# Key chain ahead of h, h in the buffer of its own transposes, and one output tile in front of attention, in a two-layer linear-attention kernel

## The reference

```python
xn = _ln(x, ln_w, ln_b)
q = xn @ Wq + bq
k = xn @ Wk + bk + (1.0 - src_mask) * -1000000.0
q = softmax(q per head, over the head's features)
k = softmax(k per head, over the tokens)
v = (xn @ Wv + bv) * src_mask
att = jnp.einsum('bnhd,bnhl->bhdl', k, v)
y = jnp.einsum('bnhd,bhdl->bnhl', q, att)
scale, shift = jnp.split(jax.nn.silu(emb) @ W_emb + b_emb, 2)
hh = _ln(y, ln2_w, ln2_b) * (1.0 + scale) + shift
out = x + jax.nn.silu(hh) @ W_out + b_out
```

## Time and profile before

| what | value |
|---|---|
| median of three runs | 903.98 us |
| profiled execution, its own time | 908.92 us |
| span of the program in it | 907.1 us |
| PE busy | 822.0 us, 91% |
| DVE, ACT, POOL busy | 703.4, 514.4, 428.5 us |
| mean granted clock of PE | 0.96 |

### The profile page before, as it was taken

One profiled execution on the slowest core, in us unless ns is written; L12 is line 12 of the kernel. 1 busy time (PEld: TensorE's weight loads), 2 busy tenths in 40 slices (PEclk: granted clock), 3 DMA queues, 4 the chain that ended last, 5 costly groups with the idle time before them and its releaser, 6 DMA issues.

```text
span 907.1 us, 13792 instructions
## 1 busy us (share of the span) xinstructions
PE 822.0 (91%) x4871; PEld 424.2 (47%) x4871; DVE 703.4 (78%) x1410; ACT 514.4 (57%) x997; POOL 428.5 (47%) x418
## 2 busy tenths in 40 slices
PE   4995998899897998999999898989989898989987
PEld 2434444354453544545454544545454454536443
DVE  5987678568696786989886887868687886868976
ACT  4663774664456665777675665555564545551431
POOL 2251684525536555657473654344254444443240
PEclk9998899999899999999999998999999999999998
DMA  9588386745565656867495838567474847557451
GB/s 319 217 161 262 73 161 181 138 94 161 110 174 115 94 158 133 207 136 184 86 179 113 155 109 152 159 121 170 94 169 111 141 138 140 128 100 157 70 116 70
DMA packets 291093, 130.53 MB, mean 144 GB/s; under 512 B 261296, under 2 KB 261680, under 8 KB 291024
## 3 DMA queue, kind: packets, MB, share of 16 engines
q1 hardware_dynamic: 288000, 124.87, 60.5%
q10 hardware_dynamic: 3024, 4.78, 1.5%
HBM read 47.74 MB, written 16.88 MB: 71 GB/s over the span
## 4 chain that ended last, share of the span: by engine, by line
PE 64%; DVE 16%; issue 10%; ACT 6%; DMA 2%; SPq 1%; POOL 0%; DVEq 0%; ACTq 0%
PE ring L493 56%; PE att_ps L493 6%; DVE sb_kt_or_y L1024 2%; ACT sb_k_or_qt L1306 2%; DVE sb_row_peak L782 1%; DVE sb_kt_or_y L1018 1%; DMA sb_w_stage<-in_L_cond_Wk 1%; DVE sb_k_or_qt L930 1%; DVE sb_kt_or_y L1029 1%; ACT sb_kq_hi L1314 1%; DVE sb_w_lo L849 1%; DVE sb_y_stats L1006 1%; DVE sb_q_sum L983 1%; DVE ring L1002 1%; ACT sb_htok L1340 1%
## 5 line engine op out<-in xcount | busy, mean ns | idle before, releaser
L493 PE MATMUL ring<-sb_w_hi,sb_xt_parts 128*128 128x512 f16 x1024 | 316.4, 386 | 0.2 <-ACT sb_v_or_q L1363 0.2
L493 PE MATMUL ring<-sb_w_lo,sb_xt_parts 128*128 128x512 f16 x512 | 197.8, 386 | 0.0
L493 PEld LDWEIGHTS ring<-sb_w_hi,sb_xt_parts 128*128 128x128 f16 x1024 | 102.4, 100 | 131.4 <-issue 15.5
L493 PE MATMUL ring<-sb_w_hi,sb_ht_parts 128*128 128x512 f16 x512 | 158.0, 383 | 1.9 <-DVE sb_v_parts L940 1.9
L493 PE MATMUL ring<-sb_xt_parts,sb_w_hi 128*128 128x512 f16 x512 | 154.9, 385 | 0.0
L1533 POOL TENSOR_TENSOR sb_htok<-sb_kt_or_y,sb_htok 128x512 f16<-128x512 f32 x60 | 75.6, 1260 | 94.4 <-ACT sb_htok L1340 93.4
L1524 POOL TENSOR_TENSOR sb_x<-sb_x,sb_bias_o 128x512 f32<-128x512 f32 x64 | 79.1, 1270 | 81.9 <-DVE sb_k_or_qt L930 76.9
L1363 ACT ACTIVATE sb_v_or_q<-ring,sb_ln_one 128x512 f32<-128x512 f32 x64 | 43.9, 686 | 107.5 <-DVE ring L965 107.5
L1549 POOL TENSOR_TENSOR sb_tanh<-sb_v_or_q,sb_kq_hi 128x512 f16<-128x512 f32 x64 | 73.7, 1161 | 55.5 <-ACT sb_kq_hi L1368 54.5
L493 PE MATMUL ring<-sb_xt_parts,sb_w_lo 128*128 128x512 f16 x256 | 98.0, 383 | 0.0
L493 PE MATMUL ring<-sb_w_lo,sb_ht_parts 128*128 128x512 f16 x256 | 97.9, 383 | 0.0
(11 more groups left out here) (214 smaller groups left out, 1513.3 us busy)
## 6 DMA issues: line engine op xcount, KB each, us to landing
out<-sb_x SPq DMA_DIRECT2D x14, 1024.0 KB, 4.5
sb_rows_now<-film_rows SPq DMA_DIRECT2D x16, 512.0 KB, 4.7
sb_x<-out SPq DMA_DIRECT2D x8, 1024.0 KB, 5.4
sb_x<-in_x SPq DMA_DIRECT2D x7, 1024.0 KB, 5.4
sb_mask_add<-mask_terms SPq DMA_DIRECT2D x15, 256.0 KB, 5.7
sb_w_stage<-in_L_cond_Wk SPq DMA_DIRECT2D x2, 1024.0 KB, 9.3
sb_w_hi<-in_L_cond_W_emb SPq DMA_DIRECT2D x1, 1536.0 KB, 12.7
sb_w_lo<-in_L_cond_W_emb SPq DMA_DIRECT2D x1, 1536.0 KB, 13.5
```

Of the source, the lines that this page charges most:

```text
L493: last = nc.tensor.matmul(out, lhs, rhs, start=(n == 0), stop=(n == len(pairs) - 1))
```

## The change

- In `keys_beside_h` and `h_beside_keys` the chain of the keys (mask, maximum, exponent, sum, high and low half) goes first, and the gates and halves of h of the unit before come between and behind; values come after both.
- SP turns the keys first and h after them, and h's turning waits for all of h (`h_lo_ready`). The keys' turning waits for h no more, because Y, z and h of every unit but the last stand in `ht_parts`, the space into which h is turned (`y_of`).
- Tile 0 of the output of u-1 stands in front of attention on PE; tiles 1 to 3 stay behind it.
- Film products (unit 2) and shift products (units 3 to 5) move from behind value tiles to behind query tiles; `turn_film` moves behind O 0, `turn_table(1)` behind K 0 of unit 3.
- On POOL `add_bias` moves behind `low_queries` and `low_attention`.
- In unit 0: the first two key tiles begin with their hi·hi products, before the low halves are there; the query weights of layer 1 are split by ACT and POOL; `attention` is split by tiles of v and `mask_attention` by column block; peak, scale and split of W_out of layer 1 are in unit 0; half of the loads of layer 2's film weights moves to unit 1.

```diff
+        def y_of(u):
+            return kt_or_y if u == LAST else ht_f32
...
             def turn_h(u):
...
+                sp.wait_ge(h_lo_ready, 4 * u)
                 turn(ht_hi.rearrange("p t c m -> p (t c) m"), flat_h[0], h_hi_ready, 4 * u, ht_hi_ready)
...
             def turn_k(u):
                 if u == 0:
-                    sp.wait_ge(w_ready[0], 8)
-                    sp.wait_ge(shift_part, 2)
-                else:
-                    sp.wait_ge(h_lo_ready, 4 * u)
+                    sp.wait_ge(q0_ready, 1)
...
+                turn_k(u)
                 turn_h(u)
-                turn_k(u)
...
             def with_k(i):
-                    if u == 1 and i == 0:
-                        pe.wait_ge(table_copied, 2)
-                        sum_w(0, O_)
+                    if u == 3 and i == 0:
+                        turn_table(1)
...
+                pe.wait_ge(ht_hi_ready, 16 * u)
+                pe.wait_ge(ht_lo_ready, 16 * u)
+                output(u - 1, (0,), with_o)
                 if shifted is not None:
                     pe.wait_ge(shift_folded, folded(1, shifted))
                 pe.wait_ge(h_ready, 4 * u)
                 attention(u)
...
-                pe.wait_ge(ht_hi_ready, 16 * u)
-                pe.wait_ge(ht_lo_ready, 16 * u)
-                output(u - 1, between=with_o)
+                output(u - 1, (1, 2, 3), with_o)
                 attend(u)
...
             def keys_beside_h(u):
                 masked_keys(u, 0)
+                masked_keys(u, 1)
                 affine(u - 1, 0)
+                masked_keys(u, 2)
+                masked_keys(u, 3)
+                key_shift(u)
                 affine(u - 1, 1)
                 gate(u - 1, 0)
                 affine(u - 1, 2)
+                affine(u - 1, 3)
+                key_sums(u)
                 gate(u - 1, 1)
+                for i in range(C):
+                    low_keys(u, i)
                 gate(u - 1, 2)
                 gate(u - 1, 3)
...
                 attended_all(u)
+                if u == 2:
+                    film_scales(1)
```

More of the change, by code:

```diff
@@ L488, in take_bank, with product @@
                 return bank(name, i, unit)
-            def product(out, pairs, ahead=lambda n: None):
+            def product(out, pairs):
                 for n, (lhs, rhs) in enumerate(pairs):
-                    ahead(n)
                     last = nc.tensor.matmul(out, lhs, rhs, start=(n == 0), stop=(n == len(pairs) - 1))
@@ L600, in attention, with first_attention @@
                 last.then_inc(att_summed, 1)
+            def first_attention():
+                pe.wait_ge(kt_hi_ready, 16)
+                pe.wait_ge(kt_lo_ready, 16)
+                for tiles in (range(T - 1), (T - 1,)):
+                    pe.wait_ge(v_lo_ready, tiles[-1] + 1)
+                    for c in range(C):
+                        f = slice(c * P, c * P + P)
+                        for t in tiles:
+                            pairs = ((tile(kt_hi, c, t), v_hi[:, t, f]), (tile(kt_hi, c, t), v_lo[:, t, f]), (tile(kt_lo, c, t), v_hi[:, t, f]))
+                            for n, (lhs, rhs) in enumerate(pairs):
+                                last = nc.tensor.matmul(att_ps[:, c, :], lhs, rhs, start=(c == t == n == 0), stop=(c == C - 1 and t == T - 1 and n == 2))
+                last.then_inc(att_summed, 1)
             def attend(u, between=lambda t: None):
@@ L970, in mask_attention @@
                 dve.wait_ge(att_summed, u + 1)
+                if u == 0:
+                    for c in range(C):
+                        nc.vector.tensor_tensor(att[:, c, :], att_ps[:, c, :], blocks[:, 0, :], ALU.mult).then_inc(att_ready, 1)
+                    return
                 if layer:
@@ L1368, in high_queries @@
                 nc.scalar.copy(kq_hi[:, t * D:t * D + D], q[:, t, :]).then_inc(q_hi_ready, 1)
+            def high_queries(u, t):
+                exponent_of_queries(u, t)
+                halve_queries(u, t)
             def high_attention(u):
-                act.wait_ge(att_ready, u + 1)
+                if u == 0:
+                    for c in range(C):
+                        act.wait_ge(att_ready, c + 1)
+                        nc.scalar.copy(att_hi[:, c, :], att[:, c, :]).then_inc(att_hi_ready, 1)
+                    return
+                act.wait_ge(att_ready, att_count(u))
                 nc.scalar.copy(att_hi[:], att[:]).then_inc(att_hi_ready, 1)
@@ L1375, in h_beside_keys @@
                 tanh_of(u - 1, 0)
+                for i in range(C):
+                    exponent_of_keys(u, i)
                 tanh_of(u - 1, 1)
+                high_keys(u)
                 high_h(u - 1, 0)
```

284 lines of the change are left out of this document (145 added, 139 removed).

## The result

The changed kernel takes 861.4 us (median of 4 runs, 860.45 to 863.32) against 903.98; the ratio is 0.954, with a 95% interval of 0.951 to 0.956. The prediction was 842 us with a range of 826 to 866.

The account below looks back on a forecast made before the run. PE was taken as the bound, its steady-unit wait set by the keys' chain. Terms -35.5 + 1.5 - 7.1 - 8.0 - 10.5 - 2.5 = -62.1 gave 846.8 us profiled, 842 us median; range 826 to 866.

Parts of the forecast that it names:

- rival 3: First units: stalls grow, eating the start's 10.5 us gain, and unit 3 pays more; 853 to 862 us, chance 0.17.
- units 3 to 6: Weight-preparing units: shift-row waits and slow products go, a new wait at sum_w comes; 219.4 to 212.3 us, -7.1.
- Steady units: Units 7 to 14: wait ahead of attention and slow clock go; 46.9 us each, -35.5 in all, +1.5 for unit 9.
- The margin of h: Steady units, ahead of O 0: h's second transpose lands at +29.9, Q ends at +31.2; margin 1.3 us, the plan's thinnest.
- shift of 4 columns: DVE, steady units: took 1.01 us beside h's low half on POOL; would come out some 0.8 us earlier without that overlap.
- O 0 in front of attention: PE, behind Q: attention then stands at +33.8; only O 1 to 3 (7.8 us) hide att's masking and halving, no wait expected.
- The sums of peaks: Units 3 to 6, at sum_w: only O 1 and O 2 (5.2 us) cover about 6.8 us of DVE work; wait 1.6 us.
- Unit 3's table: turn_table(1) behind K 0: PE waits 5.9 us for its table and loses an estimated 3.2 us of slow clock.
- Start: Up to unit 2: old waits go and K starts hi·hi, 18.7 us, less 8.2 for new waits; -10.5, the least sure term.
- Q's bank: Unit 1, third query tile: PE waits 5.4 us for its bank, freed by values that now come behind the key chain.
- Rival 1: h gates O 0: each unit waits 2 us there and pays 1.6 of slow clock; +36, 878 us, chance 0.13.
- Rival 2: Slower than before: h at O 0 5.9 us later than worked out loses the gain, 7 us gives about 915; chance 0.04.

Follow-up runs that it names:

- e12: Changed kernel with every high half of h computed four times on ACT in steps 8 to 14; 910.2 us.
- e13: e1 with SP turning h first and then the keys, the orders on DVE, ACT and POOL staying keys-first; 935.0 us.
- e3: Changed kernel with every high half of h computed twice on ACT in steps 8 to 14; 868.5 us.
- e7: Changed kernel with film_scales(1) ahead of unit 2's LayerNorm of Y and, in units 3 to 6, the sum of peaks behind O 3 instead of O 2; 842.8 us.
- e1: Changed kernel with O 0 put back behind attention, all else staying; 838.7 us.
- e9: e1 plus the edits of e5 and e6 and film_scales(1) ahead of unit 2's LayerNorm of Y; 831.2 us.
- e5: Changed kernel with ACT's second film load of layer 2 issued in unit 1 only once h's transposes have landed; 860.8 us.
- e10: Changed kernel with the second film load of layer 2 at the end of unit 1 on ACT, behind the last transposes; 851.2 us.
- e6: Changed kernel with x's statistics for unit 2 ahead of W_out's scaling and low half in unit 0, and add_bias(0) behind low_x in step 1; 856.7 us.
- e2: Kernel before with only O 0 and its waits moved in front of attention, keys, h and SP in old order; 906.8 us.

## Why the prediction was right, and where it was not

The direction, the stated range and the main mechanism held; the gain was 42.6 us where 62 were forecast. The forecast's own range, 832 to 852, was missed: 861.4 lies in the stated one only because that took in rival 3. By its own terms, in spans (forecast, measured):

| stretch | forecast | measured |
|---|---|---|
| start to unit 2 | 131.1 | 136.2 |
| unit 2 | 53.9 | 53.95 |
| units 3 to 6 | 212.3 | 220.2 |
| units 7 to 14 | 376.7 | 377.7 |
| last unit | 70.9 | 72.2 |

That makes 15.4 of the 19.4 us. The other 4 are the step from the profiled execution to the median: before, the profiled one lay 4.9 us above the median, and I took the same share off; after, it lay 0.7 above. The kernel before scatters by 1% (901.3 to 910.6) and the changed one by 0.3%. The scatter is in the clock: the mean granted clock is 0.968 in an execution of 901.6 us and 0.957 in the one of 910.6, and the difference is worth some 10 us (an estimate, 0.011 of 900 us). That it arises behind the waits of 2 to 3 us is argued, not shown; e12, with seven waits over 4 us and slow clock behind each, scatters by only 0.3%.

- **Steady units**: right, to 0.1 us in the unit (46.80 for 46.9). The reason given, the chain of the keys, was half of the truth: e13 shows that with h's pair ahead of the keys' on SP the earlier chain is worth nothing, and the kernel is 28 us slower than before. The order of SP's queue is in the change, but the prediction gave it no price.
- **The margin of h** (forecast 1.3 us): measured 0.1 in unit 12, where h's low half, issued 2.0 us behind 671.70 and 4.7 on its way, landed at 678.4 and O 0 began at 678.5. The missing 1.2 us are on POOL: the low halves of h began at +18.9 (18.3 forecast) and took 5.3 us with the gap between them (4.8 forecast), the first two of them slower beside the keys' low halves on DVE. Those took 4.12 us for four and ended at +20.6 (+19.0 forecast, at 0.8 each). The two engines did overlap, as the prediction feared. Its sentence on the shift of 4 columns points at the wrong row: the low half of h beside it ran on POOL at 692.97, not at 696.85. The expected saving came: the shift takes 0.16 us in unit 12 of the changed kernel. DVE and POOL there:

```profile
663.89 4.12 DVE L977 SCALAR_TENSOR_TENSOR sb_k_or_qt<-sb_k_or_qt,sb_k_recip,sb_kq_hi 128x512 f16<-128x512 f32 x4
666.31 2.72 POOL L1583 TENSOR_TENSOR sb_htok<-sb_ht_parts,sb_htok 128x512 f16<-128x512 f32 x2 [8.50 <-ACT sb_htok L1385]
669.34 2.27 POOL L1583 TENSOR_TENSOR sb_htok<-sb_ht_parts,sb_htok 128x512 f16<-128x512 f32 x2 [0.32 <-ACT sb_htok L1385]
```

  In unit 7 the margin was negative, 1.8 us. Waits up to 1.8 us brought no slow clock in unit 7 and in e3, where the prediction had counted on it behind any short wait; one of 2.17 in e7 brought 1.7 us.
- **O 0 in front of attention**: the step that failed. The forecast gave it 1.6 us at each of the four sums of peaks (6.4), nothing in the other units, and a thin margin for h. e1 shows that it cost 22.7 us, 15.1 of them in units 3 to 6. It took a tile of cover from behind attention, from where the sums of peaks need it, and gave none that was wanted, since the keys' transposes had landed 6 us before Q ended (672.5 against 678.5). In unit 1 it made PE stand for h while attention could have run.
- **The sums of peaks** (forecast 1.6 us each): 2.8, 3.7, 2.8 and 1.9, and 1.7 us of slow clock behind two of them. That is 4.8 us more of waiting and some 2 more of slow clock than forecast, which is most of the 7.9 that units 3 to 6 are off. The place was right, the size was not.
- **Unit 3's table**: 6.6 us for 5.9, right. e7 and e9 show that moving its small steps on DVE (`film_scales`) in front of the LayerNorm removes it.
- **Start**: `bound_film(0)` between values cost nothing (2.8 forecast), Q's bank 4.7 (5.4 forecast), but O 0 waited 8.3 us and ran 2.5 us longer. The forecast had no term for it. Behind it lies a load of 2 MB, issued 0.9 us behind h's second transpose, which then landed after 11.3 us (e5, e10). Behind the wait for Q's bank lies y's power on POOL, which stands behind 9.5 us of weights and bias; e6 puts it earlier and halves that wait.
- **Rival 1** happened in unit 1 and, for 1.8 us, in unit 7. **Rival 2** has its point about where it was put: h 5.9 us later should bring the time back to 904, and 6.4 us, in seven units only, brought 910 (e12). Its mechanism was another one, the banks of the values. **Rival 3** (853 to 862) is what came out in sum, though not quite as told: the start kept 5.4 of its 10.5 us, unit 3 paid 1.8 more, and 6.2 were lost in units 4 to 6, at sums that it did not name.

What stays open: why the clock falls behind some waits and not behind others as long, and what SP's new order alone would bring. That values behind queries or ahead of h would take e12's wait away was not tried.

## What to carry to other kernels

When a chain is moved ahead, move its place in the DMA queue with it; in e13 the chain without the queue was worse than nothing. A piece of work set in front of a wait is worth something only if the wait is still there: check what else it was covering where it stood. Before a large load is issued, look at which small transposes share its time on the DMA queues, and let it go into a gap as long as itself. A wait that the change makes shorter may only uncover the next one, as in e2, e5 and e12; so read all waits of the unit, and not only the one that was aimed at.

## What was not expected of the hardware

- Two loads of 1.5 and 0.5 MB on ACT's queue (issue to landing 8 to 14.6 us) delay a DMA transpose on SP's queue that was issued 0.9 us before them: 11.3 us for 4.5 in the changed kernel. SP is also held at the issue of a later transpose, 9.65 us in e5 against 1.9 in unit 12 and 3.3 in unit 1 of e10.
- A wait of about 2 to 3 us may or may not be followed by the half clock. In the changed kernel those of 1.79 (unit 7), 1.86 (unit 6) and 2.79 us (unit 3) were not, and that of 2.81 (unit 5) was: the 12 matmuls behind it took 4.4 us for 2.75. So were 1.85 in unit 6 of e5 and 2.17 in unit 7 of e7. The same wait can go either way: in unit 5 it is 2.81 us in e5 too, and there the full clock stays. The changed kernel's unit 5 is in the result's windows, 53.66 us at 0.97; e5's is

```profile
308.73:360.69 51.96, 49.16 (x303) 24.74 (x301) 43.89 (x87) 34.68 (x65) 31.27 (x30) 1.00 0.71 158
```

  A difference of 1.7 us between single units of two runs can therefore be chance of this kind.
